# A macaron block in exact float32 halves: half of the lower parts made by VectorE in 17 rounds of the first network, and three reordered places

## The reference

```
x = x + 0.5 * ffn(layernorm(x))
x = x + attention(layernorm(x))
x = x + 0.5 * ffn(layernorm(x))

ffn(x):   h = silu(fp4_linear(x, w_gate)) * fp4_linear(x, w_up)
          return fp4_linear(h, w_down)          # 256 -> 704 -> 256
fp4_linear(x, w) = quant(x) @ quant(w).T
quant(x): per block of 16 along the last dim: scale = max|x| / 6,
          x / scale rounded to the grid 0 .5 1 1.5 2 3 4 6, times scale
attention: complex q, k, v of width 256 (real and imaginary parts),
          softmax((qr kr + qi ki) / sqrt(256)), then v, then Wo
```

## Time and profile before

| what | value |
|---|---|
| time, median of 3 runs | 934.82 us (933.93 to 934.95) |
| the profiled execution: its time, its span | 933.85 us, 932.0 us |
| TensorE busy | 905.2 us, 97% |
| VectorE busy | 705.0 us, 76% |
| ScalarE busy | 651.6 us, 70% |
| GpSimd busy | 500.3 us, 54% |
| DMA, mean | 15 GB/s |

### The profile page before, as it was taken

One profiled execution on the slowest core, in us unless ns is written; L12 is line 12 of the kernel. 1 busy time (PEld: TensorE's weight loads), 2 busy tenths in 40 slices (PEclk: granted clock), 3 DMA queues, 4 the chain that ended last, 5 costly groups with the idle time before them and its releaser, 6 DMA issues.

```text
span 932.0 us, 16308 instructions
## 1 busy us (share of the span) xinstructions
PE 905.2 (97%) x5694; PEld 807.7 (87%) x5694; DVE 705.0 (76%) x1164; ACT 651.6 (70%) x1369; POOL 500.3 (54%) x561
## 2 busy tenths in 40 slices
PE   3999999999999999999999999999999999999997
PEld 2788888889888798998998899998988888889896
DVE  7998888998767666655474544545599999999997
ACT  5778887888784575767675576767784678566554
POOL 4556666666530154535663064546577657656562
PEclk9999999999999999999999999999999999999999
DMA  9100000000000000000000000000000000000001
GB/s 317 53 1 1 1 1 2 1 1 1 1 1 1 1 2 1 1 1 2 1 1 1 1 2 1 1 2 1 1 1 1 2 24 24 23 23 24 11 14 46
DMA packets 11953, 13.83 MB, mean 15 GB/s; under 512 B 864, under 2 KB 11104, under 8 KB 11872
## 3 DMA queue, kind: packets, MB, share of 16 engines
q1 hardware_dynamic: 11872, 12.79, 4.1%
HBM read 8.59 MB, written 4.19 MB: 14 GB/s over the span
## 4 chain that ended last, share of the span: by engine, by line
PE 83%; DVE 7%; ACT 4%; POOL 3%; issue 3%; DMA 0%; DVEq 0%; ACTq 0%; POOLq 0%
PE bank L1761 21%; PE bank L2005 19%; PE bank L1650 6%; PE bank_b L1772 6%; PE bank_b L1779 4%; PE bank L2043 4%; PE bank L2047 4%; PE bank L2045 4%; PE bank L1968 2%; PE bank L1800 2%; POOL p_lo L578 1%; PE bank_b L2047 1%; PE bank_b L2043 1%; PE bank_b L2045 1%; PE bank L1986 1%
## 5 line engine op out<-in xcount | busy, mean ns | idle before, releaser
L578 POOL TENSOR_TENSOR p_lo<-s_ring,p_hi 128x512 fp32r<-128x512 f32 x128 | 167.4, 1312 | 219.2 <-ACT p_hi L1509 219.1
L533 POOL TENSOR_TENSOR zq<-grid,s_neg 128x256 f32<-128x256 f32 (+2 forms) x184 | 173.9, 969 | 40.7 <-DVE grid L778 40.7
L940 DVE TENSOR_TENSOR top<-bank,top 128x512 f32<-128x512 f32 x112 | 77.4, 691 | 125.7 <-ACT s_ring L1493 125.7
L1761 PE MATMUL bank<-w_hi,T_hi 128*128 128x512 f32 (+1 forms) x384 | 149.2, 388 | 2.6 <-DVE z L737 1.8
L1761 PE MATMUL bank<-w_hi,T_lo 128*128 128x512 f32 (+1 forms) x384 | 143.9, 375 | 0.0
L1761 PE MATMUL bank<-w_lo,T_hi 128*128 128x512 f32 (+1 forms) x384 | 143.5, 374 | 0.0
L1493 ACT ACTIVATE s_ring<-bank 128x512 f32<-128x512 f32 x128 | 75.9, 593 | 78.1 <-PE bank L2005 78.0
L1328 ACT ACTIVATE T_hi<-bank 128x1024 fp32r<-128x1024 f32 (+1 forms) x68 | 64.6, 950 | 81.5 <-PE bank L1650 81.5
L2043 PE MATMUL bank<-v_hl,p_hi 128*128 128x258 f32 x384 | 109.9, 286 | 0.4 <-DVE x L972 0.2
L2045 PE MATMUL bank<-v_hl,p_hi 128*128 128x256 f32 x384 | 108.2, 282 | 0.0
L2047 PE MATMUL bank<-v_hl,p_lo 128*128 128x258 f32 x384 | 108.2, 282 | 0.0
(11 more groups left out here) (228 smaller groups left out, 2281.1 us busy)
## 6 DMA issues: line engine op xcount, KB each, us to landing
out<-x SPq DMA_DIRECT2D x7, 512.0 KB, 2.9
x<-in_L_attn_hidden_states SPq DMA_DIRECT2D x3, 1024.0 KB, 12.3
x<-in_L_attn_hidden_states SPq DMA_DIRECT2D x2, 512.0 KB, 6.9
wraw<-in_L_ffn_w_down SPq DMA_DIRECT2D x1, 704.0 KB, 7.4
wraw<-in_L_ffn_w_up SPq DMA_DIRECT2D x1, 640.0 KB, 4.8
wq_s<-in_L_attn_Wq SPq DMA_DIRECT2D x1, 512.0 KB, 6.4
wk_s<-in_L_attn_Wk SPq DMA_DIRECT2D x1, 512.0 KB, 7.3
wo_s<-in_L_attn_Wo SPq DMA_DIRECT2D x1, 512.0 KB, 8.3
```

Source lines behind the costliest of these rows:

```text
L533: last = nc.gpsimd.tensor_tensor(out=blocks(zq[:, to:to + hi - lo]), in0=blocks(grid[:, lo:hi]), in1=spread(s_neg[:, par, lo // BLOCK:hi / ...
L578: nc.gpsimd.tensor_tensor(out=lower_buf(n, c), in0=score_buf(n, c), in1=upper_buf(n, c).bitcast(F32), op=ALU.subtract).then_inc(plo_done, 1)
L940: nc.vector.tensor_tensor(out=top[:], in0=score_bank(c), in1=other, op=ALU.max).then_inc(top_done, 1)
L1761: last = nc.tensor.matmul(gu[:, lo:hi], lhsT=T[:, par, HK + kd, :], rhs=w[:, kd, lo:hi], start=n == 0, stop=n == len(terms) - 1)
```

## The change

Four edits. One: a rule `by_vector(f, k)` says where VectorE makes the lower parts of bank 0. In the second network that is as before (rounds 0 to 28); in the first network it now holds in rounds 4, 5, 8, 9, 12, 13, 16, 17, 20, 21 and 22 to 28, which are 17. Two: `lower_first` now stands behind `scaled` in a round, in both networks; the one written out by hand for round 0 of the second network stays in its place. Three: in round 30 of both networks `down_out` comes ahead of `late_upper`, and in round 29 of the first network `absolute(31)` comes behind `chain_rest`. Four: of the four tiles of the fourth key group VectorE normalises two and ScalarE the other two (`keys_normalised_rest`), and ScalarE makes `k_hi` of the third group one step earlier.

```diff
@@ -59,6 +59,7 @@
     ROOT = float(np.sqrt(D))
     SCALE = 1.0 / float(np.sqrt(D))
     LEAD = 4
+    FREE_FROM = NT - 2 * 5
     NCH = NT + LEAD
     NW = 6
     assert HR == 64 and G == GT * P and GT * D == 4 * I and E == 4 * P and NS == 16
@@ -267,6 +268,15 @@
         def late(k):
 
             return k >= NT - 2
+
+        def by_vector(f, k):
+
+            return isinstance(k, int) and 0 <= k < NT - 3 and (f == 1 or k >= FREE_FROM or k >= 4 and k % 4 < 2)
+
+        def vector_lowers(f, k):
+
+            whole = sum(by_vector(0, j) for j in range(NT)) if f else 0
+            return whole + sum(by_vector(f, j) for j in range(k + 1))
 
         def T_bank(k):
 
@@ -806,10 +816,10 @@
                         scales(c + 2, par)
                     if c >= -3 and chain(c + 1):
                         to_grid(c + 1)
-                    if f and hidden(c) and not late(c):
-                        lower_first(c, par)
                     if chain(c + 2):
                         scaled(c + 2)
+                    if by_vector(f, c):
+                        lower_first(c, par)
 
                 def input_statistics(c):
 
@@ -1006,7 +1016,7 @@
 
                 dve.wait_ge(o_nmr, NG + g + 1)
                 dve.wait_ge(kT_done, NG + g)
-                for a in range(4):
+                for a in range(2 if g == NG - 1 else 4):
                     t = NS + 4 * g + a
                     nc.vector.tensor_scalar(out=xn[:, a, :], in0=x[:, t, :], scalar1=nmean[:, t:t + 1],
                                             scalar2=rstd[:, t:t + 1], op0=ALU.add,
@@ -1286,6 +1296,15 @@
                 nc.scalar.activation(keys_input(0, t // 4, t % 4), x[:, t, :], ACT.Identity, scale=rstd[:, t:t + 1],
                                      bias=nmr[:, t:t + 1]).then_inc(xk_done, 1)
 
+            def keys_normalised_rest():
+
+                act.wait_ge(o_nmr, 2 * NG)
+                act.wait_ge(kT_done, 2 * NG - 1)
+                for a in (2, 3):
+                    t = NT - 4 + a
+                    nc.scalar.activation(keys_input(1, NG - 1, a), x[:, t, :], ACT.Identity, scale=rstd[:, t:t + 1],
+                                         bias=nmr[:, t:t + 1]).then_inc(xk2_done, 1)
+
             def new_statistics(t):
 
                 act.wait_ge(x_att, t + 1 if t < NT - QT else NT)
@@ -1337,7 +1356,7 @@
                 def chain_rest(k, par):
 
                     bank = bank_of(k)
-                    t = slice(4 if f and k != NT - 3 else 0, HK + KD) if hidden(k) else slice(HK, HK + KD)
+                    t = slice(4 if by_vector(f, k) else 0, HK + KD) if hidden(k) else slice(HK, HK + KD)
                     act.wait_ge(sub_done, number_lo(f, k))
                     last = nc.scalar.activation(T_lo[:, par, t, :], bank[:, t, :], ACT.Copy)
                     if hidden(k):
@@ -1369,11 +1388,13 @@
                         absolute(c + 1)
                     if f and c == 0:
                         normalise(6)
+                    if c == NT - 2:
+                        down_out(c - 1, 1 - par)
                     if late(c) and chain(c):
                         late_upper(c, par)
                     if extra and c == NT - 1:
                         keys_upper(0, 0)
-                    if hidden(c - 1) and c < NT:
+                    if hidden(c - 1) and c < NT and c != NT - 2:
                         down_out(c - 1, 1 - par)
                     if measured:
                         act.wait_ge(x_new, c - 1)
@@ -1392,12 +1413,12 @@
                         minus_mean(c - 2, c - 2)
                     if c >= 0 and hidden(c + 3):
                         silu_gate(c + 3)
-                    if extra and c == NT - 3:
-                        absolute(NT - 1)
                     if extra and c == -2:
                         query_row()
                     if chain(c) and not late(c):
                         chain_rest(c, par)
+                    if extra and c == NT - 3:
+                        absolute(NT - 1)
                     if extra and c == -2:
                         normalise(5)
                         absolute(0)
@@ -1551,8 +1572,9 @@
                     exponential(n - 1, 5)
                     p_upper(n - 1, 5)
                     exponential(n - 1, 6)
+                    keys_upper(1, 2)
                     p_upper(n - 1, 6)
-                    keys_upper(1, 2)
+                    keys_normalised_rest()
                     exponential(n - 1, 7)
                     p_upper(n - 1, 7)
                     keys_upper(1, 3)
@@ -1796,7 +1818,7 @@
 
                 pe.wait_ge(hi_done, number(f, c))
                 if hidden(c):
-                    for bank in range(1 if f and c != NT - 3 else 0, 2):
+                    for bank in range(1 if by_vector(f, c) else 0, 2):
                         last = nc.tensor.matmul(bank2[:, bank, :], lhsT=neg_ident[:],
                                                 rhs=T_hi[:, par, 4 * bank:4 * bank + 4, :],
                                                 start=False, stop=True, skip_group_check=True)
@@ -1823,8 +1845,8 @@
                     if extra and c == 0:
                         transpose_group(G1 + 2)
                         pe.wait_ge(wc["lo"], G1 + 2)
-                    if f and hidden(c - 1):
-                        pe.wait_ge(first_lo, c)
+                    if by_vector(f, c - 1):
+                        pe.wait_ge(first_lo, vector_lowers(f, c - 1))
                     if f and c == 0:
                         pe.wait_ge(x_att, NT - QT + 1)
                     transpose_chain(f, c)
@@ -1859,8 +1881,8 @@
                             pe.wait_ge(wc["lo"], len(groups))
                         project_down_first(par, dn)
                         pe.wait_ge(lo_done, number_lo(f, c))
-                        if f and c != NT - 3:
-                            pe.wait_ge(first_lo, c + 1)
+                        if by_vector(f, c):
+                            pe.wait_ge(first_lo, vector_lowers(f, c))
                         project_down_rest(par, dn)
 
                 def last_two():
```

## The result

The changed kernel takes 930.12 us, the median of 5 runs (929.08 to 931.31), against 934.95 (933.93 to 935.06) for the kernel before on the same chip. The ratio is 0.9949, with a 95% interval of 0.9938 to 0.9959, or 4.8 us less. The profiled execution is the slowest of the five, 931.31 us.

A forecast was written before the change was run, and what follows sets the result against it. TensorE, busy 905.2 of 932.0 us, was taken as the bound. Terms 3.45 + 0.1 + 0.8 + 0.1 + 0.1 = 4.55 us off 933.85 give 929.3, adjusted to a median of 929.8; range 928.2 to 931.9.

The forecast's parts named there:

- What the first edit takes from TensorE: First network: 17 rounds lose a subtraction worth 0.23 us each; 15 counted as gaining, 3.45 us.
- The wait in rounds 16 and 20: First network: `product` comes late behind a long `s_up`, TensorE's gate product waits 0.23 us, paying the round's gain back.
- `lower_first` behind `scaled`: Second network's new order: scaled values 0.05 us shorter where TensorE waits for `product`; 0.1 us gained, bounds 0 to 0.3.
- The slower rival: Second network: GpSimd's first `zq` piece delays the scaled values 0.56 us in each of 28 rounds; 938.2 us, 4 in 100.
- The fourth key group: Splitting its tiles and making `k_hi` earlier removes the transposes' wait for `k_lo`; 0.8 us gained, bounds 0.3 and 0.8.
- The rival in which the wait only changes its name: Key group gains nothing because `p_lo` 7 comes late for TensorE, while the rounds gain; 930.6 us, 15 in 100.
- The end of the second network: Earlier `down_out` moves the residual add onto VectorE's rounding and grid rows of tile 31; 0.1 us gained, bounds 0 and 0.6.
- The end of the first network: Earlier `down_out` wins 0.5 us, later `absolute(31)` may cost 0.7; 0.1 us gained, bounds -0.2 and 0.5.
- VectorE as the bound in the first network: Rival: drawn-out `s_up` makes VectorE's cycle 7.2 us in every round, first edit gives nothing; 933.2 us, 11 in 100.

The follow-up runs named there:

- experiment 1: Kernel before with only the rule `by_vector` in the first network, lower parts there behind the scaled values: 930.45 us against 934.87, ratio 0.9959.
- experiment 7: Changed kernel with VectorE making the lower parts in all rounds 4 to 28 of the first network: 931.25 us, against 929.17 for the changed kernel.
- experiment 3: Kernel before with only the key group edit (earlier `k_hi`, tiles split between VectorE and ScalarE): 932.97 us, ratio 0.9986 to the kernel before.
- Experiment 12: Changed kernel with GpSimd's residual add of tile 29 held back until `zq` of tile 31 is written, both networks: 929.36 us, ratio 0.9947 to the kernel before.
- experiment 11: Changed kernel with `absolute(31)` back in its old place: 929.23 us, ratio 0.994 to the kernel before.
- experiment 10: Changed kernel with the second network's inverse standard deviations moved behind rounds 10, 11 and 12: 930.0 us, ratio 0.9945 to the kernel before.
- experiment 9: Changed kernel with input statistics spread behind `product`, lower parts on VectorE in 16 rounds, second network's old order: 926.88 us, ratio 0.9917 to the kernel before.
- experiments 1 to 4: Kernel before with one edit each: `by_vector` rule, second network's order, key group, ends; 930.45, 934.66, 932.97, 934.38 us.

## Why the prediction was right, and where its terms were off

The forecast of 929.8 us lies 0.3 from the measured 930.12, and the change of -4.8 us stands against a sum of 4.55. The agreement is partly luck, since two errors nearly cancel. The stages give 4.9 us where the sum has 4.55. Against that, the forecast starts from an execution with the full clock (933.85) and adds 0.49 us for the median of new runs, while a run with the drop of the clock that the last section shows takes 1.0 us more, and the median of the five is such a run.

- **What the first edit takes from TensorE: 3.45 us predicted, 3.45 measured** (experiment 1), and the mechanism is shown at its two ends. Rounds 22 to 28 run at 6.91 us, so VectorE had the room that was worked out for it. Rounds 16 and 20 stay at 7.19 and 7.16, as the working said from the long `s_up`; in experiment 7, where `s_up` is short in them, they take 6.92 with the same work on VectorE. The price of a subtraction is 0.23 us as read from the pace; its duration of 400 ns would have given 17 x 0.4 = 6.8.
- **The wait in rounds 16 and 20 had the wrong name**: TensorE's waits for `product` are 7, where I wrote about 9. The working put the 0.23 us on the gate product behind `product`. TensorE is held 0.17 to 0.19 us one step earlier, at the second part of the down product, for the lower parts that the edit itself puts on the late VectorE, and starts the gate product 0.08 later behind it. The size came out since both instructions stand behind the same long `s_up`. The list of waits hardly shows it, because it counts idle time from the end of the matmul before, and that end lies 0.28 us behind its start while the next can start after 0.12.
- **`lower_first` behind `scaled`: 0.1 predicted, between 0.14 less and 0.06 more measured** over rounds 3 to 28 where no meeting comes. The step missed rounds 3 and 8: that the new order brings GpSimd forward against VectorE, by 0.05 to 0.08 us in round 3, and may let the residual add in ahead of `s_neg`, which draws the row out by 0.56 us and costs the stage 0.6 to 0.7 a meeting. The slower rival had the right kind of mechanism at the wrong row. It looked for the meeting at the scaled values in 28 rounds, where there was none.
- **The fourth key group: 0.8 predicted, 0.97 to 1.07 measured.** The wait of 0.81 went whole, and some 0.2 more came that I had no row for. Here is the changed kernel's timeline, which answers to the earlier trace rows, and behind it the last product ahead of the transposes in the kernel before:

```profile
472.38 1.74 DVE L1021 TENSOR_SCALAR xn<-x,nmean,rstd 128x256 f32<-128x256 f32 x2
...
473.02 1.01 ACT L1290 ACTIVATE k_hi<-bank 128x1024 fp32r<-128x1024 f32 x1
...
474.06 1.23 DVE L921 TENSOR_TENSOR k_lo<-bank,k_hi 128x1024 fp32r<-128x1024 f32 x1
...
474.45 1.08 ACT L1305 ACTIVATE xn<-x,nmr,rstd 128x256 f32<-128x256 f32 x2
...
475.84 0.28 PE L2069 MATMUL bank_b<-v_hl,p_lo 128*128 128x258 f32 x1
475.96 1.04 PE L1668 MATMUL bank<-ident,xn 128*128 128x128 f32 x8
```

```profile
478.61 0.28 PE L2047 MATMUL bank_b<-v_hl,p_lo 128*128 128x258 f32 x1
```

  VectorE's two tiles take 1.74 us, half as was taken; `k_lo` ends at 475.29, ScalarE's tiles at 475.53, and the transposes at 475.96 wait for neither. The rival in which the wait only changes its name fell. The term was mis-sized because it was read from the list of waits. From the last product to the transposes it was 479.70 - 478.61 = 1.09 us and is 475.96 - 475.84 = 0.12, which is 0.97 less, the whole difference of the stage; the 0.81 of the list leaves out the part in which one matmul overlaps the next. The other 0.1 of experiment 3 has no row.
- **The end of the second network: 0.1 predicted, 0.17 to 0.23 measured.** `zq`'s last piece is back to 0.22 us, and the add has moved onto the grid row, 1.30 in place of 0.89, as the working said, with 0.41 as its price instead of 0.56. Experiment 12 shows that this is what limits the step: without the meeting another 0.38 us come. The Trainium skill, in SBUF — State Buffer, section Who interferes with whom, says that such instructions exclude each other for a whole one. The trace agrees roughly: the add of 0.75 had started 0.20 ahead of the grid row, so the row would stand still for 0.55 us by that rule, and it is 0.41 longer.
- **The end of the first network: 0.1 predicted, 0.34 to 0.38 measured.** The step that was mis-sized is the balance of its two halves. `absolute(31)` costs 0.27 (experiment 11) and not up to 0.7, because VectorE is busy with tile 30 until 264.08 and only then waits; so `down_out` alone is worth about 0.6.
- **Rivals.** VectorE as the bound in the first network did not happen at 17 rounds. Experiment 7 shows how near it is: with the lower parts in the rounds of the statistics too, the waits for `product` grow by 3.2 us and the rounds lose 0.9.

## What to carry to other kernels

Price an instruction taken from a saturated TensorE by the difference in pace between two kinds of rounds that the trace already holds, and walk the helper engine's list in every kind of round, since a round in which it comes late may give nothing (here two of 17). A wait's price is read in the same way, from start to start, since the list of waits understates it. Work that nobody waits for soon (here the input statistics) belongs behind the instruction that the bound engine waits for: moving it, and the lower parts with it to the rounds that then had room, gained 2.2 us. When an operation of GpSimd is moved, by however little, look at which of VectorE's instructions with two inputs it now starts ahead of, and profile the kernel more than once before a loss of 1 us is ascribed to it.

## What the runs showed of the hardware

A meeting of GpSimd and VectorE is decided by hundredths of a microsecond. The add 0.04 us ahead of `s_neg` made it take 0.77, and so did 0.02 ahead in round 8 of the same trace (770.08 against 770.10, `s_neg` 0.79). At 0.01 ahead (experiment 10, and round 4 of the kernel before) `s_neg` stayed at 0.21 and the add took 0.81 in place of 0.73. At 0.10 behind neither was longer.

The 1.00 us ahead of round 0 is TensorE's clock. The view of windows (window, length, TensorE's busy time, granted clock, DMA share, GB/s) and the timeline show it, first in the first trace of the changed kernel, then in its second:

```profile
24.00:25.00 1.00, 1.00 (x5) 0.50 1.10 348
```

```profile
22.90 0.51 PE L1753 MATMUL bank_b<-w_hi,neg_ident 128*128 128x512 f32 x1 [2.01 <-ACT w_hi L1176]
```

```profile
24.00:25.00 1.00, 1.00 (x8) 1.00 1.11 350
```

```profile
22.95 0.51 PE L1753 MATMUL bank_b<-w_hi,neg_ident 128*128 128x512 f32 x1 [1.53 <-ACT w_hi L1176]
```

In the first trace the granted clock is 0.50 from 23.6 to 27.0 us, which is the level of 1.2 GHz, behind an idle time of 2.01 us; in the second it stays at 1.00, the level of 2.4 GHz, behind 1.53 us. The idle time alone doesn't decide it: the kernel before and experiment 3 stood idle for 2.01 and 2.02 us at the same place and kept their clock, and experiment 9 lost it behind 1.76. Of the fourteen traces nine have this drop (mean clock 0.998; start to round 0 54.7 to 55.0 us), four have none (1.000; 53.9 to 54.0), and that of experiment 9 has a longer one (0.996; 56.3). It explains much of the scatter of 1 us between the runs of one kernel. Of the 27 runs of the kernel before that stand beside experiments 1 to 4, the nine with a mean clock of 1.000 take 933.78 to 934.48 us, the twelve with 0.998 take 934.71 to 935.56, and the six with 0.996 take 936.08 to 936.29; where in the run the clock was lower is not shown for them.
